# The cross-attention stage of a twelve-stage decoder kernel rotates its PSUM work over six banks instead of eight

## The reference, cut to what matters

```python
Qn, Kn, Vn = layernorm(Q), layernorm(K), layernorm(V)      # K = V = ctx, 8 x 256 x 256
q, k, v = split_heads(Qn @ wq), split_heads(Kn @ wk), split_heads(Vn @ wv)
qn, kn = l2norm(q), l2norm(k)                               # over the 64 of each head
attn = einsum('bhqd,bhkd->bhqk', qn, kn)
out = einsum('bhqk,bhkd->bhqd', attn, v)
x = Q + out @ wo + bo
x = x + gelu(layernorm(x) @ w1 + b1) @ w2 + b2
```

## Time and profile before

| | |
|---|---|
| median of 3 runs | 2989.95 us (2988.61 to 2990.36) |
| the profiled execution, its own time | 2990.36 us |
| its span, first to last instruction | 2989.1 us |
| mean granted PE clock over the span | 0.907 |
| PE busy | 2530.3 us, 85% of the span |
| DVE busy | 1251.4 us, 42% |
| ACT busy | 817.7 us, 27% |
| POOL busy | 521.5 us, 17% |
| the stage's loop, first projection to the last `wo` | 1436.1 to 1744.1 us |
| the stage's MLP | 1750.2 to 1863.7 us |

### The profile page before, as it was taken

One profiled execution on the slowest core, in us unless ns is written; L12 is line 12 of the kernel. 1 busy time (PEld: TensorE's weight loads), 2 busy tenths in 40 slices (PEclk: granted clock), 3 DMA queues, 4 the chain that ended last, 5 costly groups with the idle time before them and its releaser, 6 DMA issues.

```text
span 2989.1 us, 34376 instructions
## 1 busy us (share of the span) xinstructions
PE 2530.3 (85%) x13778; PEld 1743.6 (58%) x13798; DVE 1251.4 (42%) x2347; ACT 817.7 (27%) x2275; POOL 521.5 (17%) x454
## 2 busy tenths in 40 slices
PE   4776999974799597887899999699956999876999
PEld 4664777763477363422466666587832688733555
DVE  7553111128288764556333322300044355656220
ACT  0110111112276161354222221122203344304220
POOL 1521222211200101211244310222220100002000
PEclk8977999996899798999899999699975999987999
DMA  4003443420100000300000000323227423100000
GB/s 147 0 29 137 165 164 143 175 83 20 45 2 15 34 1 1 117 0 26 3 1 1 0 1 1 121 82 93 72 87 295 168 87 128 36 25 1 8 8 14
DMA packets 73749, 189.48 MB, mean 63 GB/s; under 512 B 9551, under 2 KB 52949, under 8 KB 65654
## 3 DMA queue, kind: packets, MB, share of 16 engines
q1 hardware_dynamic: 65590, 169.11, 15.8%
q0 software_dynamic: 8000, 18.18, 1.9%
HBM read 143.88 MB, written 46.09 MB: 64 GB/s over the span
## 4 chain that ended last, share of the span: by engine, by line
PE 78%; DVE 14%; ACT 2%; issue 2%; POOL 1%; DMA 1%; SPq 0%; POOLq 0%; DVEq 0%; ACTq 0%
PE psum L219 42%; PE psum L3054 6%; PE psum L1248 4%; PE psum L1579 4%; PE psum L1595 4%; PE psum L1584 3%; PE psum L2100 2%; PE psum L1610 2%; PE psum L2087 2%; PE psum L3063 2%; PE psum L2774 2%; DVE stats L251 2%; DVE z L265 1%; PE psum L1575 1%; PE psum L379 1%
## 5 line engine op out<-in xcount | busy, mean ns | idle before, releaser
L219 PE MATMUL psum<-arena 128*128 128x256 f32 (+7 forms) x4172 | 1009.3, 401 | 33.7 <-DVE arena L3150 13.2
L219 PEld LDWEIGHTS psum<-arena 128*128 128x128 f32 (+4 forms) x4176 | 732.2, 182 | 300.5 <-issue 148.8
L1669 DVE TENSOR_REDUCE small<-psum 128x4 f32<-128x1024 f32 (+1 forms) x112 | 136.9, 1223 | 151.7 <-PE psum L1584 108.7
L261 POOL TENSOR_SCALAR x_moments<-x_moments 128x4 f32<-128x4 f32 x48 | 12.2, 253 | 1036.2 <-DVE x_moments L254 1036.1
L1291 DVE TENSOR_TENSOR arena<-arena,psum 128x256 f32<-128x256 f32 x138 | 57.9, 420 | 318.4 <-ACT arena L1263 318.4
L1141 POOL DMA_INDIRECT l_out<-arena,slot_tables x86 | 85.6, 995 | 494.3 <-ACT arena L1269 288.5
L3054 PE MATMUL psum<-arena 128*128 128x512 bf16 x752 | 165.4, 379 | 0.8
L1644 ACT ACTIVATE arena<-psum,small 128x128 f32<-128x128 f32 (+1 forms) x384 | 149.0, 416 | 44.4 <-DVE small L1669 44.4
L1680 DVE COPY arena<-psum 128x512 f32<-128x512 f32 x224 | 143.3, 680 | 1.6 <-PE psum L1595 1.5
L379 PE MATMUL psum<-ident,z 128*128 128x128 f32 x256 | 47.2, 345 | 111.6 <-DVE z L265 83.8
L1248 PE MATMUL psum<-arena 128*128 128x256 f32 x552 | 136.5, 392 | 0.0
(11 more groups left out here) (327 smaller groups left out, 3567.1 us busy)
## 6 DMA issues: line engine op xcount, KB each, us to landing
arena<-L_ffn_w_in SPq DMA_DIRECT2D x23, 2176.0 KB, 9.2
arena<-L_ffn_W_in SPq DMA_DIRECT2D x16, 1024.0 KB, 8.2
positions<-arena SPq DMA_DIRECT2D x16, 1024.0 KB, 3.9
arena<-positions SPq DMA_DIRECT2D x16, 1024.0 KB, 8.0
arena<-l_out SPq DMA_DIRECT2D x16, 512.0 KB, 8.1
positions<-arena SPq DMA_DIRECT2D x16, 512.0 KB, 3.4
arena<-positions SPq DMA_DIRECT2D x16, 512.0 KB, 9.0
l_out<-arena SPq DMA_DIRECT2D x2, 2048.0 KB, 13.8
```

The costliest lines, as they stand in the source:

```text
L219: last = nc.tensor.matmul(out, lhsT, rhs, start=(n == 0), stop=(n == len(pairs) - 1))
L1669: nc.vector.reduce_max(self.minus_top(h), use.bank(u).rearrange("p (h l) -> p h l", l=L), AX_X, negate=True).then_inc(self.topped.up(), 1)
```

## The change

One argument is dropped where the stage makes its `Uses`, so that the default of `Uses.__init__` (`count=6`) holds. Nothing else is edited: the order of the instructions on each engine, their number, and the waits that are written out are the same. What differs is the bank of each use, and with it which earlier use PE waits for in `take`.

```diff
-        u = self.uses = Uses(k, count=8)
+        u = self.uses = Uses(k)
```

## The result

The changed kernel takes 3036.81 us (median of 5 runs, 3034.35 to 3040.7) against 2989.95 us before, 46.9 us more; the ratio is 1.016 with a 95% interval of 1.0149 to 1.0171. 3040.6 us were forecast, 51 us more. The profiled execution has a span of 3035.1 us against 2989.1, 46.0 us more.

The account below looks back on a forecast made before the run. PE was taken to set the loop's pace; (a) and (b) 30.4 us, (c) 5.2, (d) 15 and (e) 0 summed to 51 us more, 3040.6 us, with a range of 3025 to 3053.

Parts of the forecast that it names:

- What bounds the kernel: In the stage's loop PE, busy 37.45 of 38 us, sets the pace; whatever it waits for there lengthens the kernel.
- (a): `k b+1.1` waits for a bank of `k b+1.0`, some 3.5 us six times; 30.4 us together with (b).
- (b): `oT b.2` waits for a bank of `k b+1.1`, some 1.8 us seven times; 30.4 us together with (a).
- (c): `k b+1.0` waits for DVE's late evictions of `kv b.0` and `kv b.1` in iterations 2, 4 and 6; 5.2 us.
- (d): PE's new pauses in the loop lower the granted clock to half; 15 us, bounds 0 and 23.
- (e): Ahead of the loop, a 0.93 us wait for bank 6 goes and smaller ones come; -0.3 to +0.3 us, taken as 0.
- (f): In the MLP ACT evicts a hidden bank in 0.69 us and idles 1.03; six banks are as good as eight.
- the clock holds: Rival: the loop's pauses don't lower the clock and only the waits are left; 3026 us, chance 0.09.
- the clock costs more: Rival: the loop's pauses bring longer or more half-clock stretches; 65 us more, 3055 us, chance 0.09.
- hidden: Rival: other waits of PE shrink by as much as the new ones bring; 2990 us, chance 0.03.
- faster: Rival: PE's old waits, 4.7 us at L379, `oT b.3` and `v b+1.1`, go; 2985 us, chance 0.02.

Follow-up runs that it names:

- fix_a: Six banks, but `k b+1.1` of iterations 0 to 6 gets banks 6 and 7; 2994.65 us against 2991.03 for the kernel before, ratio 1.0009.
- fix_b: Six banks, but `oT b.2` and `oT b.3` of iterations 0 to 6 get banks 6 and 7; 3019.53 us against 2991.03 before, ratio 1.0097.
- fix_c: Six banks, but `kv b.0` and `kv b.1` get banks 6 and 7; 3030.72 us against 2991.03 for the kernel before, ratio 1.0132.
- short_power: Changed kernel with POOL's power taken of 4 of the 16 heads only; 2990.56 us against 2990.56 for the kernel before, ratio 1.0001.
- filled: Changed kernel with extra matmuls on PE in the pauses ahead of `k b+1.1` and `k b+1.0`; 3025.52 us against 2991.03 before, ratio 1.0114.
- count7: Kernel before with a ring of seven banks instead of eight; 2999.22 us against 2990.56, ratio 1.0028.
- planned_six: Changed kernel with banks 0 to 5 handed out in the loop; 2986.89 us against 2990.56 for the kernel before, ratio 0.9989.
- six_ahead: Six banks for the turn of the context ahead of the loop only, eight from the first projection on; 2987.8 us against 2991.04 before, ratio 0.9989.

## Why the prediction was right

**What bounds the kernel** held: PE sets the loop's pace, and what was taken off its waits came off the loop, as fix_a, fix_b and fix_c show one by one. In the time of the whole kernel it comes out within a few us only (fix_c: 12.1 us in the loop, 6.1 in the time).

**(a)** 3.5 us and a restart of 0.16 were forecast for `k b+1.1`; six waits of 3.48 us were measured, and fix_a and short_power tie them to the chain of `k b+1.0`.

**(b)** 1.77 us were forecast, 1.66 measured (1.43 in iteration 0). fix_b removes them. From one first `qT` to the next, iteration 0 became 1.8 us longer (1.8 forecast), iteration 1 by 6.27 and iteration 5 by 7.05; less 1.7 us for a fall each, that is 4.57 and 5.35, where 4.51 and 5.28 were forecast for (a) and (b).

**(c)** 0.45, 2.18 and 2.18 us were forecast, 0.44, 2.17 and 2.17 measured. fix_c removes them. The sum of (a), (b) and (c), 35.6 us, stands against 36.4 us in filled.

**(d)** 15 us were forecast, 13.4 measured (filled). Two terms in it were mis-sized and nearly cancel: a pause of 3.5 us costs the short stretch, 1.7 us, not my middle of 2.3, which is 3.6 us too much for six; and both pauses of 2.2 us lowered the clock, 3.4 us where I had written 1. That the sum is only 1.6 us off is luck. For the second term the trace of the kernel before had a row that I left out: PE was idle for 2.21 us until 2362.43, and the clock fell behind it. The pauses of (b) were rightly taken as too short: no fall comes behind one.

```profile
2362.43 0.39 PE L1575 MATMUL psum<-causal 128*128 128x256 bf16 x2 [2.21 <-ACT z L1644]
```

```profile
2364.00:2367.40 3.40, 3.40 (x17) 3.40 (x18) 0.00 (x0) 1.17 (x8) 0.00 (x0) 0.50 0.00 0
```

The rule of the Trainium skill ("Perfetto Trace Analysis", Matmul Optimizations) that matmuls should run back to back agrees with filled, where work in the pauses gives back 13.4 us. Its rule on using all eight banks, on the same page of the Trainium skill, is borne out here only for a ring: count7 costs 9 us, and planned_six, on six, nothing.

**(e)** 0 was taken, with bounds of 0.3 us, and in the changed kernel that held, though not only by the waits that were added up. Counted from the first turn of the context (1418.40, before 1418.29), the first projection started 1.2 us earlier (1435.04): 0.45 us by the two waits, as forecast, and 0.7 because the first turn of `z` ran at a higher granted clock (0.85 against 0.50), its row taking 1.22 us instead of 1.94. At the first `qT` 0.2 us were left. What took 1.0 us back lies in the four projections between, 16.21 us long against 15.21. In six_ahead they take 15.80: so 0.4 us are the wait of `v0.1` for `k0.0` that six banks bring (0.1 to 0.3 were forecast). The other 0.6 us are half clock, which covers some 4.1 us of them in six_ahead (mean 0.52 over the first 4.22 us) and 2.8 before (0.57 over 3.29). The chain of `q0.1`, which was said to start no earlier, does start earlier and hides nothing: from the first query projection to the first `qT` it is 15.98 us in all three kernels.

**(f)** held: in the MLP ACT idles for 59.4 us before its evictions against 60.5, and PE has no new wait there.

The forecast's 51 us against 46.9: 49.8 us are in the loop, 50.6 were forecast for it; most of the difference lies in stages with the same code. Of the rivals, "the clock holds" is refuted by filled, "the clock costs more" by the length of the eight falls, 3.4 us each, "hidden" and "faster" by the list of waits. The mechanism that should have made it faster is there, and planned_six shows its size: 2.4 us in the loop, where the rival had 3.8 for it (its 0.93 us at L379 lie ahead of the loop).

## What to carry to other kernels

Count for each PSUM use how long it stays full and how much PE work lies between it and the next use of its bank; a ring is good or bad by that distance, and one use with a long chain over three engines can make seven banks cost 9 us, six 47, and six well placed none. Let a use that is emptied quickly follow itself, give the slow ones the longest way round, and price each pause of PE with what the clock does behind it: here 1.7 us for every fall of 3.4 us, over a quarter of the loss.

## What the runs showed of the hardware

Pauses of equal length between equal work don't all lower the granted clock. 3.48 us did so six times of six in the changed kernel, three of six in fix_b, four of six in fix_c; 2.17 us did so two times of two, one of two in fix_b and one of two in fix_a. The half clock lasted 3.4 or 6.8 us each time. What decides between equal pauses no run here tried. And POOL's power of 128x16 takes 2.90 us, of 128x4 some 1.0 us (the median of 32 in short_power is 1.007).
